# The decay of a delta-rule scan moves from ScalarE into the scan's first VectorE product, and sigmoids are made from tanh

## The reference

```python
a = jax.nn.sigmoid(x @ Wa.T + ba)
bgate = jax.nn.sigmoid(x @ Wb.T + bb)
def step(S, inp):                       # over the 512 tokens
    qt, kt, vt, at, bt = inp
    Sk = jnp.einsum('bhde,bhe->bhd', S, kt)
    S_new = at * S - at * bt * outer(Sk, kt) + bt * outer(vt, kt)
    ot = jnp.einsum('bhd,bhde->bhe', qt, S_new)
    return (S_new, ot)
...
# experts, in both layers: the best two of 8 or 16, weights that sum to 1
weights, idx = jax.lax.top_k(probs, TOP_K)
weights = weights / jnp.sum(weights, axis=-1, keepdims=True)
```

## Time and profile before

| | |
|---|---|
| times of three runs | 1351.15, 1360.18, 1360.09 us; median 1360.09 |
| the profiled execution's own time | 1352.62 us |
| its span | 1350.9 us |
| busy in the span | PE 73%, DVE 63%, ACT 46%, POOL 33% |
| scans 0 to 3, first to last state | 75.3 to 160.8, 162.6 to 245.6, 248.5 to 350.1, 353.0 to 426.0 us |
| ACT_TABLE_LOAD | 1.28 us each, 17 of them before 500 us |

### The profile page before, as it was taken

How to read it: one execution, slowest core, us unless ns; L and a number is a source line. 1 busy time by engine, 2 the same in 40 slices (tenths; PEclk the granted TensorE clock), 3 DMA queues, 4 the chain that set the end, 5 groups by cost and what they waited for, 6 DMA issues and landing times.

```text
span 1350.9 us, 18007 instructions
## 1 busy us (share of the span) xinstructions
PE 989.0 (73%) x5924; PEld 600.3 (44%) x5924; DVE 846.5 (63%) x2008; ACT 623.9 (46%) x1485; POOL 442.6 (33%) x636
## 2 busy tenths in 40 slices
PE   5563074985886896888788888878788878775682
PEld 3231032443453454333334555544556545544582
DVE  1386978858988332675666566766566666624452
ACT  3435253464444253154444456643556534663272
POOL 0201352634633323022442331363241444422413
PEclk9776595996997998787888899987999988998796
DMA  7000000000000001000000323212134003331372
GB/s 221 1 0 1 0 0 1 1 1 35 1 1 1 1 0 36 1 1 1 1 1 1 114 71 105 75 36 92 33 111 122 29 18 120 106 107 46 125 218 80
DMA packets 53885, 64.67 MB, mean 48 GB/s; under 512 B 6544, under 2 KB 38304, under 8 KB 53792
## 3 DMA queue, kind: packets, MB, share of 16 engines
q1 hardware_dynamic: 51744, 59.33, 14.6%
q0 software_dynamic: 2048, 4.20, 1.0%
HBM read 52.83 MB, written 10.68 MB: 47 GB/s over the span
## 4 chain that ended last, share of the span: by engine, by line
PE 46%; DVE 19%; issue 13%; ACT 11%; POOL 8%; DMA 2%; SPq 0%; DVEq 0%; POOLq 0%; ACTq 0%
PE banks L701 8%; PE banks L844 4%; PE banks L758 4%; DVE MX L1323 3%; PE banks L554 3%; PE banks L776 3%; POOL oms L1796 3%; PE banks L748 2%; PE banks L818 2%; PE banks L711 2%; PE banks L714 2%; PE banks L606 2%; POOL QX L1695 2%; PE banks L723 2%; ACT PT L1620 1%
## 5 line engine op out<-in xcount | busy, mean ns | idle before, releaser
L1323 DVE TENSOR_REDUCE MX<-banks 128x4 f32<-128x512 f32 (+2 forms) x192 | 199.3, 1044 | 87.2 <-PE banks L818 86.5
L1774 POOL TENSOR_SCALAR_AFFINE_SELECT PT<-PT 128x256 f32<-128x256 f32 x256 | 107.0, 432 | 419.4 <-ACT PT L1620 419.1
L1620 ACT ACTIVATE PT<-banks 128x768 f32<-128x768 f32 (+1 forms) x192 | 167.9, 876 | 92.6 <-PE banks L776 91.5
L701 PE MATMUL banks<-xgT,wg 128*128 128x128 f32 x736 | 106.3, 290 | 36.1 <-ACT ysb L1581 29.5
L701 PEld LDWEIGHTS banks<-xgT,wg 128*128 128x128 f32 x736 | 92.5, 198 | 57.7 <-issue 53.0
L844 PE MATMUL banks<-PT,VA 128*17 128x512 f32 (+3 forms) x1024 | 98.4, 482 | 13.6 <-DVE on L1346 13.6
L783 PE MATMUL banks<-KS,QS 32*128 32x512 f32 (+3 forms) x512 | 96.7, 421 | 14.7 <-DVE MX L1323 12.3
L776 PE MATMUL banks<-QS,KS 32*128 32x128 f32 (+3 forms) x512 | 91.7, 407 | 15.0 <-ACT PT L1620 9.6
L748 PE MATMUL banks<-w,hid 128*128 128x128 f32 x512 | 76.1, 296 | 30.6 <-DVE hid L1268 28.5
L748 PEld LDWEIGHTS banks<-w,hid 128*128 128x128 f32 x512 | 69.6, 206 | 63.3 <-DVE hid L1268 43.9
L1272 DVE SCALAR_TENSOR_TENSOR sil<-sil,yh 128x256 f32<-128x256 f32 x124 | 53.4, 431 | 62.7 <-ACT sil L1567 62.4
(11 more groups left out here) (256 smaller groups left out, 2120.8 us busy)
## 6 DMA issues: line engine op xcount, KB each, us to landing
wg<-in_ffn_dram SPq DMA_DIRECT2D x92, 386.0 KB, 3.4
xg<-xs SPq DMA_DIRECT2D x20, 256.0 KB, 3.1
yb<-ysb SPq DMA_DIRECT2D x20, 256.0 KB, 3.9
w<-in_ffn_w_dram SPq DMA_DIRECT2D x12, 256.0 KB, 5.0
xs<-zt SPq DMA_DIRECT2D x1, 1472.0 KB, 11.1
x<-in_L_attn_x_dram SPq DMA_DIRECT2D x4, 256.0 KB, 5.0
out_dram<-x SPq DMA_DIRECT2D x16, 64.0 KB, 1.5
wmod<-in_L_wmod_dram SPq DMA_DIRECT2D x2, 384.0 KB, 4.1
```

Of the source, the lines that this page charges most:

```text
L701: mm = e.matmul(ps[:, at:at + cols], w, h, start=True, stop=True)
L1323: v_mx.at(e.tensor_reduce(MX[n % 2][:, u:u + nm, qb % 2, 2 * pair:2 * pair + 2, 24].rearrange("p s i -> p i s"), p4, AX.X, ALU.max, negate ...
L1620: a_p.at(e.activation(PT[q % 3][:, 2 * pair:2 * pair + 2, :], where["score", q, pair][:, :, 0:n], ACT.Exp, scale=ISQ8))
L1774: ins = e.affine_select(out=pt, in_=pt, compare_op=ALU.is_ge, fill=0.0, base=0, pattern=[[0, 2], [1, 128]], channel_multiplier=-1)
```

## The change

1. In the scan, each chunk of `XU` gets a fifth row of 8 equal elements, the decay. The first product has 5 rows instead of 4 (160 elements), and its fifth row is the decayed state, which lies in one buffer (`TS`) in front of the second product. ACT's L1518 is gone; ACT writes the fifth rows once for each group (`gm` on ACT, `a_gx`).
2. The second product is laid out as token, then key element, so that it reads KT with a step of 4 elements (16 bytes), and the second sum reads its 5 addends 8 elements (32 bytes) apart; both were contiguous.
3. `values` may be two steps ahead instead of three (three buffers instead of four).
4. sigmoid(x) is 0.5 + 0.5 tanh(x/2): for the decays (no reciprocal), and for the two gates, from the difference of the two best scores. The tables are loaded 4 times instead of 18.
5. On DVE `ab` has a lateness of 6 instead of 1, `route` 2 instead of 1, `o_x` 2 instead of 1. ACT's part of routing moves from part 0 to part 2. `otok` and `xt` lie in OL.

```diff
-    DVE=dict(mod=1.0, gate=1.0, ab=1.0, up=5.0, route=1.0, o_x=1.0),
+    DVE=dict(mod=1.0, gate=1.0, ab=6.0, up=5.0, route=2.0, o_x=2.0),
...
+        XUf = [sb(f"XU{i}", [128, 32 * 56 + 4], where=st) for i in range(2)]
+        XUc = [t[:, 0:32 * 56].rearrange("p (c x) -> p c x", x=56) for t in XUf]
...
+        TS = [sb(f"TS{i}", [128, 4, 76], where=st) for i in range(3)]
+        T0 = [t[:, :, 0:45].rearrange("p r (j e) -> p r j e", e=9)[:, :, :, 0:8] for t in TS]
+        T1 = [t[:, :, 0:36].rearrange("p r (j e) -> p r j e", e=9) for t in TS]
+        T2 = [t[:, :, 44:76].rearrange("p r (j e) -> p r j e", e=8) for t in TS]
+        T3 = [t[:, :, 36:76].rearrange("p r (j e) -> p r e j", e=8) for t in TS]
...
                 elif part == 4:
...
-                    n = v_own.at(e.tensor_tensor(Q, M, gq2[:, :, 0:E], ALU.mult))
-                    v.wait_ge(v_own, n)
-                    rt["n"] = v_own.at(e.tensor_reduce(gm[:, 0, :], Q, AX.X, ALU.add))
+                    v_gk.at(e.tensor_scalar(gk[r % 2][:, 0, :], gd[:, :], -0.5, 0.5, ALU.mult, ALU.add))
+                    v_gk.at(e.tensor_scalar(gk[r % 2][:, 1, :], gd[:, :], 0.5, 0.5, ALU.mult, ALU.add))
...
             def share(g):
...
-                n = v_own.at(e.tensor_scalar(abf, abf, 1.0, None, ALU.add))
-                v.wait_ge(v_own, n)
-                v_dec.at(e.reciprocal(abf, abf))
+                v_dec.at(e.tensor_scalar(abf, abf, 0.5, 0.5, ALU.mult, ALU.add))
...
             def scan(g, c):
...
-                n = v_own.at(e.tensor_tensor(T1[k1][:, :, :, 0:8], S_[:, c, :, :].unsqueeze(2).broadcast_to([128, 4, 4, 8]),
-                                             XU[:, c, :, 0:8].unsqueeze(1).broadcast_to([128, 4, 4, 8]), ALU.mult))
+                n = v_own.at(e.tensor_tensor(T0[k1], S_[:, c, :, :].unsqueeze(2).broadcast_to([128, 4, 5, 8]),
+                                             U5.unsqueeze(1).broadcast_to([128, 4, 5, 8]), ALU.mult))
...
-                n = v_own.at(e.tensor_tensor(t2[:, :, :, 0:4], W_[:, c, :, :].unsqueeze(2).broadcast_to([128, 4, 8, 4]),
-                                             KT[:, c, :, :].unsqueeze(1).broadcast_to([128, 4, 8, 4]), ALU.mult))
+                n = v_own.at(e.tensor_tensor(T2[k1], W_[:, c, :, :].unsqueeze(3).broadcast_to([128, 4, 4, 8]),
+                                             KT[:, c, :, :].rearrange("p e j -> p j e").unsqueeze(1)
+                                             .broadcast_to([128, 4, 4, 8]), ALU.mult))
                 v.wait_ge(v_own, n)
-                v.wait_ge(a_ts, j + 1)
...
-                v_s.at(e.tensor_reduce(Sn, t2[:, :, :, :], AX.X, ALU.add))
+                v_s.at(e.tensor_reduce(Sn, T3[k1], AX.X, ALU.add))
...
             def decay(g):
                 a.wait_ge(v_ab, g + 1)
-                a_dx.at(e.activation(ab[:, g, :, :], ab[:, g, :, :], ACT.Exp, scale=-1.0))
+                a_dx.at(e.activation(ab[:, g, :, :], ab[:, g, :, :], ACT.Tanh, scale=0.5))
...
+            def gm_(g):
+                a.wait_ge(v_gm, g + 1)
+                a.wait_ge(v_s, 32 * (g - 1))
+                a_gx.at(e.activation(XUc[g % 2][:, :, 48:56], GMb[g % 2][:, :, 3:4].broadcast_to([128, 32, 8]), ACT.Copy))
...
-                a.wait_ge(v_gm, g + 1)
-                a.wait_ge(g_zero, 1)
-                a.wait_ge(v_s, j)
-                a_ts.at(e.activation(T2[c % 2][:, :, :, 4], Sb[g % 2][:, c, :, :], ACT.Copy, scale=GMb[g % 2][:, c, 3:4]))
-                if c + 3 < 32:
-                    values(j + 3)
+                if c + 2 < 32:
+                    values(j + 2)
```

More of the change, by code:

```diff
@@ L274, in build @@
         gq = sb("gq", [128, 4, 16])
-        gq2 = sb("gq2", [128, 4, 16])
+        gd = sb("gd", [128, 4])
+        gk = [sb(f"gk{i}", [128, 2, 4]) for i in range(2)]
         go = sb("go", [128, 2, 4, 16])
@@ L334, in build @@
         GMb = [sb(f"GM{i}", [128, 32, 4], where=st) for i in range(2)]
-        XUb = [sb(f"XU{i}", [128, 32, 4, 12], where=st) for i in range(2)]
+        XUf = [sb(f"XU{i}", [128, 32 * 56 + 4], where=st) for i in range(2)]
+        XUc = [t[:, 0:32 * 56].rearrange("p (c x) -> p c x", x=56) for t in XUf]
+        XUb = [t[:, :, 0:48].rearrange("p c (j x) -> p c j x", x=12) for t in XUc]
         KTb = [sb(f"KT{i}", [128, 32, 8, 4], where=st) for i in range(2)]
-        T1 = [sb(f"T1{i}", [128, 4, 4, 9], where=st) for i in range(4)]
-        T2 = [sb(f"T2{i}", [128, 4, 8, 5], where=st) for i in range(2)]
+        TS = [sb(f"TS{i}", [128, 4, 76], where=st) for i in range(3)]
[3 more added lines that the diff above has]
+        T3 = [t[:, :, 36:76].rearrange("p r (j e) -> p r e j", e=8) for t in TS]
         Wb = [sb(f"Wb{i}", [128, 32, 4, 4], where=st) for i in range(2)]
@@ L344, in build @@
         PR = sb("PR", [128, 32, 3, 12], where=st)
-        otok = sb("otok", [128, 4, 8, 16], where=st)
+        otok = OL[:, :, :, :].rearrange("p c j e -> p (c j e)")[:, 0:512].rearrange("p (b x h) -> p b x h", x=8, h=16)
         oT = sb("oT", [128, 512], where=st)
@@ L365, in build @@
         gX = sb("gX", [128, 2, 4, 16])
-        gk = [sb(f"gk{i}", [128, 2, 4]) for i in range(2)]
         gc = sb("gc", [128, 16, 4])
@@ L1241, in o_ol @@
                 v.wait_ge(p_ol, g)
+                v.wait_ge(v_x1, g)
                 v_ol.at(e.tensor_tensor(
@@ L1434, in route @@
             def route(r, part):
-                if part == 0:
-                    E = 8 if r < 4 else 16
+                if part == 2:
                     a.wait_ge(v_rd, r + 1)
-                    a_rx.at(e.activation(gq2[:, :, 0:E], gq2[:, :, 0:E], ACT.Exp))
+                    a_rx.at(e.activation(gd[:, :], gd[:, :], ACT.Tanh, scale=0.5))
             def qkv(g, w):
@@ L1512, in scan @@
                 if c == 0:
-                    for k in range(3):
-                        values(j + k)
-                a.wait_ge(v_gm, g + 1)
-                a.wait_ge(g_zero, 1)
-                a.wait_ge(v_s, j)
-                a_ts.at(e.activation(T2[c % 2][:, :, :, 4], Sb[g % 2][:, c, :, :], ACT.Copy, scale=GMb[g % 2][:, c, 3:4]))
-                if c + 3 < 32:
-                    values(j + 3)
+                    values(j)
+                    values(j + 1)
+                if c + 2 < 32:
+                    values(j + 2)
             def o_sum(g, part):
@@ L1726, in o_ol @@
                 g_.wait_ge(p_ol, g)
+                g_.wait_ge(v_x1, g)
                 g_ol.at(e.tensor_tensor(
```

62 lines of the change are left out of this document (26 added, 36 removed).

## The result

| | before | changed |
|---|---|---|
| median of 20 runs, us | 1352.07 | 1362.80 |
| lowest to highest | 1347.95 to 1361.18 | 1351.38 to 1367.08 |
| ratio, 95% interval | | 1.0056 (1.0039 to 1.0074) |
| span of the profiled execution | 1350.9 | 1359.3 |

The change makes the kernel slower by about 0.6%, 7.5 us by the ratio, which goes by all runs; the means are 7.7 us apart, the medians 10.7. I had forecast 1343, with 1322 to 1362 as the range. The sign is wrong, and the time is just outside the range.

The account below looks back on a forecast made before the run. No engine bounds a whole scan: DVE's dependent chain in scans 0 and 3, often PE with ACT in scan 2. Gains of 18.9 less costs of 5.6 made 13.3; 1339.3 plus 3.7 gave about 1343 us, range 1322 to 1362.

Parts of the forecast that it names:

- The price of the two steps: DVE's strided reads in each scan step: 50 ns more for the second product, 0 for the second sum.
- The upper bound: Most a scan step could lengthen on DVE: 37 + 112 + 269 = 418 ns, the sum's share from ACT's strided writes.
- The number of steps on the path: Half of the 128 scan steps, 64, lie where DVE sets the pace; at 87 ns each they cost 5.6 us.
- The gains in the scans: Less DVE lateness and stalls, and fewer table loads: 2.6, 5.3, 5.3 and 3.4 us in scans 0 to 3.
- (a): Rival: DVE bounds everywhere, all 38.1 us of stalls come back, 1319.5 or 1323 us; scan 2 over 10 shorter; chance 0.17.
- Tanh: Table loads removed on ACT: 1.3 us ahead of scan 0, 1.0 in scan 1, 0.9 in scan 2, 1.0 behind the last.
- First product: DVE's first product in each scan step, 160 elements instead of 128: 37 ns longer.
- values two steps ahead: In the scans, waits of the first sum on `values` were to stay under 5 us in all.
- what lies behind the scans: Experts behind the last scan and layer 1 were to keep their lengths within 2 us.
- (b): Rival: other waits in the scans take over, only 3 to 6 us gained, 1346 to 1349 or 1350 to 1353; chance 0.18.
- (c): Rival: DVE's strided reads cost as on ACT, 356 ns a step; slower from 295 ns; 1360 to 1368 us; chance 0.15.
- The base: Starting time of the whole kernel: profiled 1352.6 us, with 3.7 added, half its 7.5 below the three-run median.

Follow-up runs that it names:

- e4: Changed kernel with 52 extra DVE instructions ahead of all others, to time contiguous and strided operands; 128-element product 292 ns contiguous, 92 ns more at a 4-element step.
- e2: Kernel before with only the layout of both strided readings added; ratio 1.0151 to the kernel before, scans 371.4 us against 350.7.
- e10: Changed kernel with KT stored by rows, both products in the slower loop order in steps 0 to 19 of each scan; ratio 1.0052, scans 357.9 us.
- e11: Changed kernel with KT stored by rows, both products in the slower loop order in steps 20 to 31 of each scan; ratio 1.0036, scans 358.5 us.
- e3: Changed kernel with both strided readings made contiguous, wrong elements summed into a scratch tile; ratio 0.9898 to the kernel before, scans 340.8 us.

## Why the prediction was wrong

- **The price of the two steps: wrong, and decisive.** I took 50 ns for the second product and 0 for the second sum. Measured: 90 and 117 in the scans, and 83 and 118 with POOL idle (e4). For the sum I leaned on L1125, 189 ns against 182, and read 7 ns as nothing. It is a scalar product of 32 elements, in which most of the price doesn't show (6 ns in e4). For the product I leaned on L1136, 28 ns for 32 elements or 112 for 128, and divided it over its operands. The row was near enough; the dividing was the error, since the price isn't shared among operands (92 ns with one, 98 with an input and the output). The upper bound, taken from ACT's strided writes at 1.84 times, was 418 ns a step in all; 34 + 90 + 117 = 241 is a little above its middle. The rule of the Trainium skill that I weighed, in SBUF — State Buffer, section "Door 1: The DMA port swizzle", says that an access which crosses into a new line of 16 bytes pays. The trace agrees, with 292 ns at a step of 8 bytes and 384 at 16, and so doesn't bear out that 4 fp32 elements are still free, as the same section has it. I set the rule aside on account of an instruction too short to show it.
- **The number of steps on the path: wrong.** I took 64. e2 says 20.7/0.207 = 100; e10 and e11 say 9.9/0.211 = 47 of the 80 ahead of AB and all 48 behind it, 95. The picture behind the 64 was that a step ahead of a wait costs nothing, because the wait shrinks by as much. In e10 that is so in scan 0 only. And in e2, which keeps the stalls on the decayed state, those stalls took up about 6 us of 26.5 and left 20.7. So the stalls are poor cover for longer steps even where they stand, and in the change 38.1 us of them are gone. Why they cover so little these runs don't show; that ACT writes the decayed state only after the state of the step before, so that a longer step makes ACT late as well, is a likely reason that was not tested. With 100 steps, my own price of 87 ns would have made 8.7 us instead of 5.6.
- **The gains in the scans: right in kind, somewhat too large.** For a change without the steps I had 16.6 less 64 x 0.037, so 14.2 us in the scans; e3 has 9.9. In the changed kernel the first instruction on AB in scan 0 starts at 125.10 instead of 128.86, 3.8 us sooner where I had 2 to 3. Counted from the start of the scans that is only 1.6 us, and it stands behind a wait of 6.9 us. In scans 1 and 2 the addition of the bias comes as soon as L648 is through, or after another instruction:

```profile
196.40 2.05 PE L648 MATMUL banks<-wo,oT 128*128 128x128 f32 x8 [0.69 <-ACT oT L1531]
198.48 0.69 DVE L1245 TENSOR_TENSOR OL<-banks,bo 128x512 f32<-128x512 f32 x1 [1.72 <-PE banks L648]
...
300.14 1.05 PE L648 MATMUL banks<-wo,oT 128*128 128x128 f32 x8
301.91 0.68 DVE L1245 TENSOR_TENSOR OL<-banks,bo 128x512 f32<-128x512 f32 x1
```

  In scan 1 that is 1.2 us earlier than in the earlier trace rows, where it was 2.2 us late; but L648 itself ran for 2.05 us instead of 1.21 and ended 1.0 us later in the execution. In scan 2 it is later than in the earlier trace rows, and the whole scan is 1.3 us longer, where (a) wanted it over 10 us shorter.
- **Tanh: right.** 4.2 us were in the sum (1.3, 1.0, 0.9, 1.0), 7 were measured, with an interval of 3 to 11. In the scans 1.9 were summed and 2.5 came; outside them 2.3 and 4.5. Where the other 2.2 lie was not looked for.
- **First product, values two steps ahead, what lies behind the scans: right.** 34 ns against 37; 2.9 us of waits for the values, where under 5 were allowed; 924.9 and 925.1 us behind the scans in the two profiles, though one kernel's own profiles differ there by up to 12 us. The experts behind the last scan, from 440 to 500 us before and from 448 to 508 in the changed kernel, stand at 1.00 of the granted clock in both.
- **The rivals.** (a), DVE as the bound everywhere, is out: without the steps only 9.9 us of scan came back. (b), other waits, is true in part (6.9 us for AB, 9.6 ahead of `hid`), but did not decide. (c) is what happened, by its mechanism, at a lower price and on more steps. Its point of decision, 295 ns a step, was wrong with the 64: at 100 steps it is 18.9/100 = 189 ns. The chance of 0.10 above 1373.7 doesn't fit (c)'s own times, which end at 1368.
- **The base.** I added 3.7 us because the median of three runs lay 7.5 above the profiled execution. The median of 20 is 1352.07, the profiled execution's own time, so the 3.7 should have been 0. It brought the forecast nearer to the result by luck.

Put together, from the forecast of -13.3: the steps cost 20.4 instead of 3.2, which is 17.2 more; the gains in the scans are 4.3 smaller; tanh brings 2.2 more outside the scans than summed. -13.3 + 17.2 + 4.3 - 2.2 = +6.0, where +7.5 was measured; the difference is within the intervals.

## What to carry to other kernels

Price a strided operand on an instruction of the kind and length that it will have: a scalar product of 32 elements paid 6 ns where a sum of 160 paid 118. Don't divide a measured price over operands without a run that shows it divides. When a change removes stalls and makes the instructions between them longer, don't count the longer instructions as hidden by the stalls; run the kernel before with the longer instructions alone, as e2 does, and see how much comes through. Once an operand's layout is free to choose, as KT's was, let its producer write it in the order of the loop that reads it.

## What the runs showed of the hardware

- DVE on fp32, in e4: a step of 2 elements (8 bytes) is free, 4 (16 bytes) costs 0.7 ns an element, 8 the same in the sum. On a product of 128 one operand at a step of 4, input or output, costs 83 to 92 ns, an input and the output 98. On a scalar product of 32 it is 6 ns.
- DVE beside POOL: in the kernel before every product of the scans over 293 ns has a POOL instruction beside it. The 46 second products with one take 590 ns on average, the others 292; the second sum takes 320 either way.
- The scans of one kernel, KT by rows, repeat to 0.3 us (348.3, 348.0, 348.3); those of the changed kernel to 2.2 (361.1, 358.9). In the three profiles of KT by rows the scans start between 72.7 and 76.5 us and what lies behind them takes 921.1 to 933.1 us. A change within a stage is better measured there than by the whole.
